# Linear attention of a two-layer decoder: one more projection ahead of the first values product of each half, with the gate kept in one buffer per half

## The reference, cut to what matters

```
qkv = silu(hidden_states @ qkv_w.T)             # q, k, v of 32 heads
scores = einsum(q, k) * decay                   # causal, one decay per head
attn = einsum(scores, v)
xf = attn * rsqrt(mean(attn * attn) + eps)      # over all 4096 channels of a token
gate = sigmoid(hidden_states @ gate_w.T)
out = (gate * (norm_w * xf)) @ out_w.T
```

## Time and profile before

| | before |
|---|---|
| median of 3 runs | 2882.61 us |
| profiled execution: span from its first to its last instruction | 2876.0 us |
| what the median run has beyond that span | 6.6 us |
| TensorE busy, whole span | 2627.4 us (91%) |
| DVE / ACT / POOL busy, whole span | 1803.5 / 967.0 / 1038.0 us |
| linear attention, stretch 1370 to 2560 us: TensorE busy | 1102.0 of 1190.0 us |
| linear attention: DVE / ACT / POOL busy | 766.4 / 421.1 / 368.3 us |
| mean granted TensorE clock in that stretch | 0.97 |

### The profile page before, as it was taken

The page is one execution under the profiler, slowest core; times in us unless marked ns, Lnnn a source line. Parts: engine busy times, 40 slices in busy tenths (PEclk is TensorE's granted clock), DMA queues, the critical chain, the costliest instruction groups (busy, mean ns, idle before and its releaser), DMA issues.

```text
span 2876.0 us, 43863 instructions
## 1 busy us (share of the span) xinstructions
PE 2627.4 (91%) x14411; PEld 2228.6 (77%) x14411; DVE 1803.5 (63%) x3756; ACT 967.0 (34%) x2732; POOL 1038.0 (36%) x584
## 2 busy tenths in 40 slices
PE   5998999999999999968999999999999999958998
PEld 4786888888888888856888888888888888846665
DVE  6446566666666666665666666666666666666665
ACT  1111333333333333311333333333333333314663
POOL 3236333433334333321333333333332323344661
PEclk9998999999999999978999999999999999959998
DMA  2112111211112111100111111111111101110000
GB/s 100 52 51 81 45 58 44 72 44 57 45 45 72 44 58 44 52 24 30 53 35 36 37 38 38 38 38 37 34 36 34 35 31 37 39 44 1 1 0 30
DMA packets 37555, 121.62 MB, mean 42 GB/s; under 512 B 4984, under 2 KB 7416, under 8 KB 37504
## 3 DMA queue, kind: packets, MB, share of 16 engines
q1 hardware_dynamic: 37504, 120.97, 12.3%
HBM read 118.86 MB, written 2.10 MB: 42 GB/s over the span
## 4 chain that ended last, share of the span: by engine, by line
PE 73%; DVE 14%; issue 7%; ACT 3%; POOL 2%; SPq 0%; DVEq 0%; DMA 0%; ACTq 0%; POOLq 0%
PE pj L492 14%; PE pj L494 14%; PE pj L493 14%; PE ou L492 6%; PE ou L494 5%; PE ou L493 5%; DVE act_lo L1411 3%; PE sc L492 2%; PE sc L493 2%; PE sc L494 2%; PE pv L494 2%; PE pv L493 2%; PE pv L492 2%; DVE probs L1160 1%; DVE probs L1324 1%
## 5 line engine op out<-in xcount | busy, mean ns | idle before, releaser
L380 POOL TENSOR_TENSOR w_hi<-raw,one 128x1024 fp32r<-128x1024 f32 x175 | 339.4, 1939 | 1659.1 <-PE pj L494 856.4
L492 PE MATMUL pj<-xt_hi,w_hi 128*128 128x512 f32 (+2 forms) x1296 | 527.4, 407 | 15.6 <-DVE act_lo L1117 10.4
L494 PE MATMUL pj<-xt_hi,w_lo 128*128 128x512 f32 (+2 forms) x1296 | 510.7, 394 | 0.0
L493 PE MATMUL pj<-xt_lo,w_hi 128*128 128x512 f32 (+2 forms) x1296 | 510.2, 394 | 0.0
L382 POOL TENSOR_TENSOR w_lo<-raw,w_hi 128x1024 fp32r<-128x1024 f32 x175 | 432.2, 2470 | 13.7
L492 PE MATMUL ou<-w_hi,act_hi 128*128 128x512 f32 x684 | 276.8, 405 | 48.5 <-DVE act_lo L1463 39.7
L492 PEld LDWEIGHTS pj<-xt_hi,w_hi 128*128 128x128 f32 x1296 | 251.3, 194 | 67.4 <-DVE act_lo L1117 14.1
L494 PEld LDWEIGHTS pj<-xt_hi,w_lo 128*128 128x128 f32 x1296 | 250.6, 193 | 55.1
L1443 DVE TENSOR_TENSOR silu<-silu,pj 128x512 f32<-128x512 f32 (+1 forms) x256 | 141.6, 553 | 238.0 <-ACT silu L1022 237.6
L493 PEld LDWEIGHTS pj<-xt_lo,w_hi 128*128 128x128 f32 x1296 | 252.0, 194 | 44.8
L494 PE MATMUL ou<-w_hi,act_lo 128*128 128x512 f32 x684 | 270.4, 395 | 0.0
(11 more groups left out here) (251 smaller groups left out, 6263.3 us busy)
## 6 DMA issues: line engine op xcount, KB each, us to landing
raw<-in_l1a_w SPq DMA_DIRECT2D x80, 512.0 KB, 3.4
raw<-in_l0x_w SPq DMA_DIRECT2D x64, 512.0 KB, 4.6
side<-in_side SPq DMA_DIRECT2D x32, 512.0 KB, 4.0
raw<-in_ffn_w SPq DMA_DIRECT2D x15, 512.0 KB, 3.3
side<-in_ctx_t SPq DMA_DIRECT2D x8, 512.0 KB, 3.3
raw<-in_l1x_w SPq DMA_DIRECT2D x7, 512.0 KB, 3.4
raw<-in_l0f_w SPq DMA_DIRECT2D x6, 512.0 KB, 4.3
raw<-in_taylor_w SPq DMA_DIRECT2D x5, 512.0 KB, 6.6
```

Source lines behind the costliest of these rows:

```text
L380: pool.tensor_tensor(WH[:, s, :], RAW[:, s, :], ONE[:].broadcast_to((P, PIECE)), ALU.mult).then_inc(w_hi[s], 1)
L492: pe.matmul(out, wh, xh, start=first, stop=False)
L493: pe.matmul(out, wh, xl, start=False, stop=False)
L494: return pe.matmul(out, wl, xh, start=False, stop=last)
```

## The change

The order of steps in the linear attention is another. F1 stands ahead of V0, and from there on F2 stands where F1 stood, and so on; F5 comes ahead of O3, so that S follows O3 directly. The gate of a half is kept in a buffer of its own: before, both halves shared `gate` [128, 2, 512]; now it is [128, 4, 512], with two rows for each half, and lies over the mask's memory and no longer over the context's. ACT's wait ahead of the gate's sigmoid is for the values products of the half before the last, HB (4) fewer. The instructions are the same in number and shape.

```
-L1A_STEPS = [("F", 0), ("V", 0), ("F", 1), ("O", 0), ("V", 1), ("F", 2), ("O", 1), ("V", 2), ("F", 3), ("O", 2),
-             ("V", 3), ("F", 4), ("O", 3), ("F", 5), ("S", 0), ("F", 6), ("F", 7), ("F", 8), ("F", 9)]
+L1A_STEPS = [("F", 0), ("F", 1), ("V", 0), ("F", 2), ("O", 0), ("V", 1), ("F", 3), ("O", 1), ("V", 2), ("F", 4),
+             ("O", 2), ("V", 3), ("F", 5), ("O", 3), ("S", 0), ("F", 6), ("F", 7), ("F", 8), ("F", 9)]
...
-            G = shared.enter_context(nc.sbuf_tensor("gate", [P, 2, 512], FP32))
...
+        with ExitStack() as shared:
+            G = shared.enter_context(nc.sbuf_tensor("gate", [P, 4, 512], FP32))
...
-                            act.wait_ge(pv_done, i * B + (PV["l1a"] + hf * HB + 1))
-                            act.activation(G[:, n - 4, :], pj[bank][:], ACT.Sigmoid).then_inc(la_sg, 1)
+                            act.wait_ge(pv_done, i * B + (PV["l1a"] + hf * HB + 1 - HB))
+                            act.activation(G[:, 2 * hf + n - 4, :], pj[bank][:], ACT.Sigmoid).then_inc(la_sg, 1)
...
-                            g = G[:, n - 4, :]
+                            g = G[:, 2 * hf + n - 4, :]
...
-                                          G[:, :, n * S:(n + 1) * S], ALU.mult).then_inc(pv_done, 1)
+                                          G[:, 2 * hf:2 * hf + 2, n * S:(n + 1) * S], ALU.mult).then_inc(pv_done, 1)
```

## The result

The changed kernel takes 2918.5 us, the median of 4 runs (2917.53 to 2918.73), against 2884.7 us for the kernel before (4 runs, 2882.2 to 2887.48). The ratio is 1.0121, 95% interval 1.0105 to 1.0136: 34 us slower, where 21 us were forecast. The span of its profiled execution is 2916.6 us, its own time 2918.39.

A forecast was written before the change was run, and what follows sets the result against it. TensorE, busy nearly throughout, was taken as the bound. Waits 0, clock falls +30 and earlier falls -7.5 gave +22 us on the 2876.0 us span, 2898, plus 6.6 makes 2904 us; own range 2892 to 2916, with rivals 2868 to 2922.

The forecast's parts named there:

- rival 4: Clock at O0: all waits are followed by a fall, or the falls last longer: 2920 to 2930 us; 6%.
- Half A, 3.8 us to 2.4: Half A: V0's wait goes, but POOL holds a low part ahead of V0's chain; O0 waits 2.4 us, 1.4 gained.
- Half B, 1.0 to 2.4: Half B: POOL's split of slot 0 holds V0's sum of squares; O0 loses 2.4 us in place of 1.0.
- Waits together at nothing: TensorE's waits in both halves, without the clock: 15 x (1.4 - 1.4), about 0 us.
- The rival by 0.16 us: Half A: F0's low part gets in ahead of POOL's fourth instruction, O0 starts at 10.75: 2881 us; 13%.
- The clock, 30 us: Behind O0 of each half: 17 to 18 of 31 idle times followed by a clock fall costing 1.7 us each.
- 7.5 us of before: Falls behind V0's waits in the kernel before, 8 x 0.3 + 3 x 1.7 us, subtracted in the sum.
- 6.6 us: Whole kernel: distance of the median run above the profiled span, added to 2898 us to give 2904.

The follow-up runs named there:

- POOL's new order: POOL splits the gate weights ahead of the value weights; in the changed kernel: 2862.35 us, ratio 0.9935; with the old order of steps: 2884.64 us, ratio 1.0026.
- DVE's (1.00 us): Changed kernel with the first low part of the queries behind V0's three instructions on DVE, POOL untouched: 2843.31 us, ratio 0.9874.
- the run with slot 0 alone later: Changed kernel, POOL's gate weights split ahead of the value weights and slot 0's split one projection later, behind F2 of half B: 2818.3 us, ratio 0.98.
- the run with TensorE kept at work: Changed kernel with 8 more matmuls of 128x512, never read, ahead of the wait of each half's first output product: 2865.53 us, ratio 0.9953.

## Why the prediction was right

The change was called slower, by 21 us; it is slower by 34, within the range (2868 to 2922). The 2918.5 us lie above the forecast's own 2892 to 2916, between it and rival 4: the waits came as forecast, and one term, the clock's, was mis-sized.

- **Half A, 3.8 us to 2.4.** Right. O0 was put at 11.3 us after F0 and stands at 11.28; the low part was to end at 9.76 and ends at 9.82. That its order ahead of V0's chain and POOL's hold make the wait is shown from both sides, by POOL's new order (0.10 us) and by DVE's (1.00 us).
- **Half B, 1.0 to 2.4.** Right. O0 stands at 11.32, and no wait appeared at O1.
- **Waits together at nothing.** Right: 72.27 us a group with the falls taken away, where a group of before without a fall took 72.37 (from one V0 to the next).
- **The rival by 0.16 us**, a low part that gets in ahead of POOL's fourth instruction, did not occur. The distance was 0.08 to 0.09 us, and POOL had it in all 15 halves A. The rival was a real one: at 0.02 us, in the run with slot 0 alone later, DVE did get in.
- **A reading that does not hold.** The prediction says that no DVE row with two SBUF operands ends within a POOL instruction. Its own rows have one: the low part of half B ends at 1689.56, and POOL's second instruction runs from 1689.09. Nothing in the sum hangs on it, but it is a second way in for DVE, between two POOL instructions.
- **The clock, 30 us.** The mechanism was right, the term too small. The mean clock of 1370 to 2560 us went from 0.97 to 0.96. I took 17 to 18 falls of 31 at 1.7 us. There were 27, at 1.57 us: 42 us, and 2.88 us a group x 15.5 = 45 us by the run with TensorE kept at work. With the 7.5 us of before that makes 35 to 37, where the medians give 34 and the two profiled spans 41, of which 32 lie in the 14 groups. What failed is the share: I scaled it from 11 of 15 at 2.33 us down for a shorter idle time, where it rose to 27 of 31. The falls are not independent draws. In the record they follow one another from half to half at 37.5 us, which is what a half takes on the average; from 1476 us on there are five in a row and then three times seven, with one half A without a fall between. Why the share rose and why the misses come so regularly stays open: no run varied the spacing alone.
- **What lies around the span.** I added 6.6 us, the distance of before's median from its profiled span, to the changed kernel as well. There the profiled execution's own time is 1.8 us above its span. The other 4.8 us were a matter of before alone: its executions lie between 2872 and 2887 us at mean clocks from 0.964 to 0.954, the profiled one was among the faster, and 11 of 15 is the count of that one. The four of the changed kernel lie within 1.2 us of each other. Span against span the forecast was 2898 and the result 2916.6, so the sum was short by some 19 us, of which the falls at O0 make 12 to 15. The rest was not followed, and by luck the 4.8 us hid a part of it.

## What to carry to other kernels

Distance between producer and consumer on TensorE buys nothing if the same table moves instructions ahead of the chain on another engine: lay out the in-order queue of each engine over the new order, and see which instruction is held by whom. Where GpSimd and VectorE share work, ask first when the GpSimd instructions run; here their order and the schedule of TensorE each cost when changed alone and gained together. Moving one held instruction behind the chain on VectorE gained too, without any change on GpSimd. And where a wait of TensorE is followed by a slower clock, look whether a second wait hides it, as O0's did before; once that is gone, the slower clock is paid in full.

## What the runs showed of the hardware that was not expected

- How often the clock fell goes with the idle time before it. Within the groups, no idle time of 1.00, 1.67 or 1.75 us was followed by a fall. Those of 2.33 ahead of V0 were in 11 of 15 cases before and in 15 of 15 with the new POOL order, those of 2.24 at O0 of half A in 11 of 15, and those of 2.27 at O0 of half B in 15 of 15 and, with the new POOL order, 14 of 15. The O0 of the very last half B stands idle 2.12 us in six kernels, and in five of them the clock fell. No run has an idle time between 1.75 and 2.12 us in its groups, and from 2.12 us on its length alone does not decide. With useless matmuls in such a wait TensorE kept 2.4 GHz (granted clock 1.00 over 1000 us).
- Which of POOL and DVE is held can hang on 0.01 us: of two instructions that start nearly together, DVE's was held 0.03 us behind POOL's in seven groups, and got in 0.005 to 0.02 us behind it in eight. That made 1.3 us in the length of a group.
- A held DVE instruction gets in between the two POOL instructions of a split, though these are only 0.07 us apart: in half B of before it ends 0.47 us after POOL's second has started (1689.09), and that one then takes 2.73 us in place of 2.38 to 2.41.
- The gate's product with `norm_w`, a `tensor_scalar` with its tensor in SBUF, is held as well: 1.57 us beside POOL (the row at 1960.41 above); otherwise it takes 0.49.
